# Second attention: the shared experts' second product with the activations stationary, and the rank bank moved

## The reference, cut to what matters

```python
x = x + L0_xattn(layernorm(x), ctx)      # softmax attention, 16 heads
x = x + L0_ffn(layernorm(x))             # 8 experts, top 2
x = x + L1_xattn(layernorm(x), ctx)      # attention with softmax on q and k, no score matrix
x = x + L1_ffn(layernorm(x))             # 8 experts, top 2, and 2 shared experts

# in L1_ffn
sh = gelu(einsum('td,sdh->sth', xf, sW1) + sb1[:, None, :])      # 2 shared, hidden 512
shared = (einsum('sth,shd->std', sh, sW2) + sb2[:, None, :]).mean(axis=0)
gates = xf @ rW + rb                                             # top 2 of 8, softmax of the two
out = shared + moe
```

## Time and profile before

| | |
|---|---|
| median of 3 runs | 737.65 us (734.78 to 743.04) |
| the profiled execution | 741.51 us, span 739.5 us |
| busy in the span | PE 677.2 us, DVE 476.6, POOL 380.2, ACT 316.1 |
| mean granted clock of PE | 0.949 |

### The profile page before, as it was taken

How to read it: one execution, slowest core, us unless ns; L and a number is a source line. 1 busy time by engine, 2 the same in 40 slices (tenths; PEclk the granted TensorE clock), 3 DMA queues, 4 the chain that set the end, 5 groups by cost and what they waited for, 6 DMA issues and landing times.

```text
span 739.5 us, 15744 instructions
## 1 busy us (share of the span) xinstructions
PE 677.2 (92%) x5140; PEld 503.8 (68%) x5140; DVE 476.6 (64%) x1380; ACT 316.1 (43%) x665; POOL 380.2 (51%) x502
## 2 busy tenths in 40 slices
PE   7999999999998889999978799999999799999990
PEld 3566666666667669899956455555554499999990
DVE  3576887878787758887756777777565233333336
ACT  3444455445433233232213366666654344444440
POOL 5313175576557625666740277666655245545552
PEclk9999999999999779999996899999999799999996
DMA  6811111120201558988790000000001778877769
GB/s 174 268 19 10 11 29 28 25 36 19 36 20 37 153 138 266 268 265 260 216 257 0 1 29 30 23 23 26 31 25 41 217 238 262 272 240 228 229 209 285
DMA packets 102119, 91.34 MB, mean 124 GB/s; under 512 B 52952, under 2 KB 85848, under 8 KB 101720
## 3 DMA queue, kind: packets, MB, share of 16 engines
q1 hardware_dynamic: 86375, 68.80, 34.3%
q0 software_dynamic: 8640, 17.84, 6.8%
q10 hardware_dynamic: 7025, 3.70, 1.8%
HBM read 69.13 MB, written 22.72 MB: 124 GB/s over the span
## 4 chain that ended last, share of the span: by engine, by line
PE 68%; DVE 14%; DMA 6%; ACT 4%; issue 3%; POOL 2%; SPq 2%; POOLq 0%; DVEq 0%; ACTq 0%
PE pair L1373 38%; PE pair L1679 11%; PE pair L1376 8%; PE pair L1731 5%; DVE sm L1126 4%; DVE smax L1122 4%; DMA xr<-xs_sorted 2%; PE pair L1479 2%; DMA y_tok<-ysb,xr 2%; PE pair L1494 2%; DMA xa<-y_tok 1%; PE pair L1414 1%; PE pair L1410 1%; POOL y_tok L629 1%; DVE bns L1072 1%
## 5 line engine op out<-in xcount | busy, mean ns | idle before, releaser
L629 POOL DMA_INDIRECT y_tok<-ysb,xr x142 | 136.3, 960 | 121.9 <-DVE ysb L1042 93.1
L556 POOL DMA_INDIRECT xs_sorted<-xa,slot_i x128 | 131.3, 1026 | 89.1 <-DVE slot_i L949 54.1
L1373 PE MATMUL pair<-xT,w_all 128*128 128x256 f32 (+1 forms) x640 | 139.9, 363 | 0.0
L1373 PEld LDWEIGHTS pair<-xT,w_all 128*128 128x128 f32 x640 | 110.4, 198 | 9.6
L1679 PEld LDWEIGHTS pair<-w_all,hT 128*128 128x128 f32 x852 | 107.1, 193 | 3.6 <-issue 0.4
L1679 PE MATMUL pair<-w_all,hT 128*128 128x128 f32 x852 | 108.8, 276 | 0.2 <-DVE hT L1029 0.2
L806 ACT ACTIVATE hT<-pair,w_all 128x256 f32<-128x256 f32 (+1 forms) x160 | 62.7, 447 | 76.3 <-PE pair L1373 75.6
L1021 DVE COPY xT<-pair 128x256 f32<-128x256 f32 (+1 forms) x80 | 31.5, 394 | 94.1 <-PE pair L1376 87.2
L1373 PE MATMUL pair<-xeT_all,w_sh 128*128 128x512 f32 x128 | 69.4, 625 | 0.0
L823 ACT ACTIVATE hS<-pair,w_sh 128x512 f32<-128x512 f32 x64 | 44.0, 687 | 55.9 <-PE pair L1373 55.1
L1122 DVE TENSOR_REDUCE smax<-pair 128x8 f32<-128x616 f32 x64 | 50.4, 788 | 25.7 <-PE pair L1373 25.2
(11 more groups left out here) (199 smaller groups left out, 1119.5 us busy)
## 6 DMA issues: line engine op xcount, KB each, us to landing
w_all<-in_w SPq DMA_DIRECT2D x40, 578.0 KB
w_all<-in_w SPq DMA_DIRECT2D x40, 450.0 KB
xa<-y_tok SPq DMA_DIRECT2D x32, 256.0 KB, 5.2
xr<-xs_sorted SPq DMA_DIRECT2D x62, 130.0 KB
y_tok<-ysb,xr POOLq DMA_INDIRECT x142
xs_sorted<-xa,slot_i POOLq DMA_INDIRECT x128
out<-x_sb ACTq DMA_DIRECT2D x8, 256.0 KB, 3.5
xs_sorted<-in_pads SPq DMA_DIRECT2D x12, 130.0 KB, 4.3
```

The lines of the kernel that those rows point to most:

```text
L556: g.indirect_dma_start(xs_dram[l], bass.IndirectOffsetOnAxis(ap=slot_i[:, i:i + 1], axis=0), xa[:, GT * c + j // TOPK, j % TOPK, :], None) ...
L629: g.indirect_dma_start(y_dram[l], bass.IndirectOffsetOnAxis(ap=xr[u % NXR][:, t, P:P + 1].bitcast(I32), axis=0), ysb[u % NYB][:, t, :], None)\
L1373: return mm(out_, l_, r_, start=True, stop=True)
```

## The change: what it does

The second product exchanges its operands: the activations `hS` are the weights (128 hidden x 128 tokens, four tiles), a 128x128 block of `w_sh` streams through, and the result has tokens on its partitions. The four tiles share a bank; only the first product of a group opens it. Groups alternate between banks 6 and 7. ACT's copy and PE's transposes go. DVE scales and adds the bank to `x_sb`, then adds the bias, which is now laid out over 128 partitions and 128 columns in `w_sh` (and prepared there once). The ranks of this layer move to bank 2, which `nums` uses too: `values(u)` waits for the slots of group `u - 2`, and the column sum of `u - 1` comes behind `out_turned(u)`, the ranks behind the up-projection of `fill(12)`. For the last group both stay where they were. Ahead of the second routed part PE waits for the add of group 6, whose bank it takes.

```diff
-WSC = NSH * B1 + NSH * NC1 + NSH
+WSC = NSH * B1 + NSH * NC1 + NSH * P
...
         def rank_bank(l):
-            return bank[6 + l]
+            return bank[6 - 4 * l]
...
-                def shared_out(u):
-                    act.wait_ge(S("sdown_step"), NC1S * (u + 1))
...
-                    s_.activation(yS[u % 2][:], bank[6][:], ACT.Identity, bias=sb2[:], scale=1.0 / NSH)\
-                        .then_inc(S("sy_ready"), 1)
...
             def shared_add(g):
-                dve.wait_ge(S("sT_done"), g + 1)
-                xg = x_sb[:, GT * g:GT * (g + 1), :].rearrange("p t d -> p (t d)")
-                v.tensor_tensor(xg, xg, bank[7][:], ALU.add).then_inc(S("sx_added"), 1)
+                dve.wait_ge(S("sdown_step"), NC1S * (g + 1))
+                xg = x_sb[:, GT * g:GT * (g + 1), :]
+                link(v.scalar_tensor_tensor(xg, bank[6 + g % 2].rearrange("p (t d) -> p t d", d=P), 1.0 / NSH, xg,
+                                            ALU.mult, ALU.add))
+                v.tensor_tensor(xg, xg, sb2.unsqueeze(1).to_broadcast([P, GT, P]), ALU.add).then_inc(S("sx_added"), 1)
...
                     if c == 0:
-                        after(pe, S("sy_ready"), g)
+                        after(pe, S("sx_added"), g - 1)
                     wd = s * B1 + UP + k * P
-                    mm(bank[6][:], w_sh[:, wd:wd + P], hS[i % 4][:], start=(c == 0), stop=(c == NC1S - 1))\
-                        .then_inc(S("sdown_step"), 1)
-
-                def shared_turn(u):
-                    pe.wait_ge(S("sy_ready"), u + 1)
-                    pe.wait_ge(S("slots"), NCH + min(u + 2, NGRP))
-                    after(pe, S("sx_added"), u)
                     for t in range(GT):
-                        last = turn(tile(bank[7], t), tile(yS[u % 2], t))
-                    last.then_inc(S("sT_done"), 1)
+                        last = mm(tile(bank[6 + g % 2], t), tile(hS[i % 4], t), w_sh[:, wd:wd + P],
+                                  start=(c == 0 and t == 0), stop=(c == NC1S - 1 and t == GT - 1))
+                    last.then_inc(S("sdown_step"), 1)
...
                 def values(u):
...
+                    if u > 1:
+                        pe.wait_ge(S("slots"), NCH + u - 1)
...
                     fill(8, 9)
-                    if live(u - 1):
-                        after(pe, S("sx_added"), u - 2)
-                        column_sums(1, u - 1)
+                    if u == NGRP:
+                        column_sums(1, U_LAST)
                     fill(10, 11)
+                    if u == NGRP:
+                        ranks(1, U_LAST)
                     if live(u):
                         out_turned(u)
-                    if live(u - 1):
+                    if live(u - 1) and live(u):
+                        column_sums(1, u - 1)
+                    fill(12)
+                    if live(u - 1) and live(u):
                         ranks(1, u - 1)
-                    fill(12)
                     if live(u):
                         project(u)
-                    if live(u - 2):
-                        shared_turn(u - 2)
                     fill(13, 14, 15)
             attention1()
+            pe.wait_ge(S("sx_added"), NGRP - 1)
             pe.wait_ge(S("emap"), 2)
             routed(1)
```

More of the change, by code:

```diff
@@ L240, in build @@
         w_sh = sb("w_sh", [P, WSC])
-        sb2 = sb("sb2", [P, 1])
+        sb2 = w_sh[:, NSH * (B1 + NC1):NSH * (B1 + NC1) + P]
         cst = sb("cst", [P, K_N])
@@ L833, in turned @@
                     copy_out(dst, bank[0][:]).then_inc(S(name), 1)
-                def shared_out(u):
-                    act.wait_ge(S("sdown_step"), NC1S * (u + 1))
-                    if u == 0:
-                        act.wait_ge(S("sb2_ready"), 1)
-                    after(act, S("sT_done"), u - 1)
-                    s_.activation(yS[u % 2][:], bank[6][:], ACT.Identity, bias=sb2[:], scale=1.0 / NSH)\
-                        .then_inc(S("sy_ready"), 1)
                 for u in range(-1, NGRP + 2):
@@ L867, in attention1 @@
                     gelu(u, 8)
-                    if live(u - 2):
-                        shared_out(u - 2)
                     gelu(u, 10)
@@ L1247, in shared_bias @@
                 dve.wait_ge(S("ws_in"), 16)
-                sbc = NSH * (B1 + NC1)
-                link(v.tensor_tensor(sb2[:], w_sh[:, sbc:sbc + 1], w_sh[:, sbc + 1:sbc + 2], ALU.add))
-                v.tensor_scalar(sb2[:], sb2[:], 1.0 / NSH, None, ALU.mult).then_inc(S("sb2_ready"), 1)
+                sbc = NSH * (B1 + NC1) + P
+                link(v.tensor_tensor(sb2, sb2, w_sh[:, sbc:sbc + P], ALU.add))
+                link(v.tensor_scalar(sb2, sb2, 1.0 / NSH, None, ALU.mult))
             def attention1():
@@ L1863 @@
                         + [cols(i[M1 + "sb1"])[s] for s in range(NSH)]
-                        + [cols(i[M1 + "sb2"])[s] for s in range(NSH)], axis=1)
+                        + [np.broadcast_to(i[M1 + "sb2"][s][None, :], (P, P)) for s in range(NSH)], axis=1)
     wa = np.concatenate([i[n][:, None] for n in (A0 + "bq", A0 + "bk", A0 + "bv", A1 + "bv")]
```

## The result

The changed kernel takes 742.56 us (median; 736.26 to 745.94), the one before, run beside it, 738.38 (733.52 to 744.57): a ratio of 1.0048, 95% interval 1.0029 to 1.0066 (the quotient of the two medians is 1.0057; the ratios in this text are estimates with an interval and need not be that quotient). The changed kernel is slower by about half a per cent. The forecast, 741.1 for a median of 737.65, is a ratio of 1.0047. The profiled executions can't be set against each other as wholes: the one after has the longer loop and is shorter, 740.42 us (span 738.4) against 741.51, since its loop began some 6 us earlier. The first transposes of the exponentials stand at 389.00 instead of 395.37 (in the other profiles of this study, with either form of the loop, between 391.9 and 395.9), those of group 1 at 408.60 instead of 414.52.

A forecast was written before the change was run, and what follows sets the result against it. PE looked like the bound, with a second path through DVE, POOL and ACT only 0.22 us slack. 0.50 + 0.8 + 1.1 + 0.9 + 0.16 = +3.5 us on 737.65 gave 741.1 us; range 732.1 to 747.7.

The forecast's parts named there:

- The second product's step: PE, shared experts' second product with operands exchanged: +0.04 us for each of 64 steps, +0.32 per group.
- The rival of weight loads that aren't hidden: PE, second product: six more loads each paid like a product, +0.66 a step, +42 us, 780; chance 0.02.
- Transposes go, PE's balance -0.11 per group: PE, each group: four transposes saved, -0.43 us, against +0.32 for the second product's steps.
- The new waits cost nothing: Second attention: products waiting for earlier groups' slots or add, and the wait ahead of the routed part, cost nothing.
- Slots 1.0 later, half swallowed by the third scatter, 0.22 of slack: DVE to POOL to ACT: scatters end 0.50 us later; after slack the exponential comes +0.28 per hand-over.
- PE alone is the bound: Second attention loop: later slots don't matter, so 734.6 us with free steps or 736.9 with dearer ones; chance 0.25.
- the scatters are caught again: POOL, third scatter held off by DVE's bias add: total +6.5 us, 744.2, or +7.5, 745.2; chance 0.23.
- The last group's kept input +0.9: Last group, DVE's kept input feeding PE's transposes: some 0.1 us spare, no bias add beside the scatters, +0.9.
- Four dearer steps +0.16: PE, last group, from the kept input's transposes to its ranks: four dearer second-product steps, +0.16 us.
- one at +0.8: One loop hand-over where the third scatter already takes 0.96 us, so nothing is swallowed: 1.0 - 0.22 = +0.8.
- The first hand-over, +0.50: First group-to-group hand-over of the second attention loop: no slack, so the scatters' whole +0.50 us is lost.
- the clock as a rival: PE's half-clock stretch ahead of the routed part: return one or two us sooner or later, 1.5 us either side.

The follow-up runs named there:

- order_alone: Kernel before with only the column sums and ranks moved later (shared transposes half a step later): 743.73 us against 739.53, ratio 1.0050.
- no_bias_add: Changed kernel without DVE's second add, so the shared experts' second bias is missing: 741.62 us, ratio 1.0036 to the kernel before.
- the split alone: Changed kernel with two instead of three scatters ahead of the next inverse deviation on POOL: 738.36 us, ratio 0.9992 to the kernel before.
- tail_early: Changed kernel with two scatters ahead of the inverse deviation (one in the last group) and the last group's transposes, logits, sums and ranks earlier: 734.75 us, ratio 0.9950.

## Why the prediction was right

The forecast followed the right path: the sums and ranks come later, POOL's scatters with them, and DVE's query reaches ACT behind the end of the table load. That it came out at the measured ratio to the fourth place is luck, since the interval is 1.0029 to 1.0066 and two terms of the sum were wrong. By its steps:

- *The second product's step*: +0.04 to 0.90 (the two rows, 0.85 and 0.90, give 0.05); measured 0.89. The rival of weight loads that aren't hidden (1.5 us a step, 780) fell.
- *Transposes go, PE's balance -0.11 per group*: PE's work per period fell by 0.15.
- *DVE's second add is hidden*: 0.30 of 129.03 us came back when it was taken away, 0.24 of it by a gap elsewhere.
- *The new waits cost nothing*: in the stretch from 409 to 600 PE waited for the copy of the exponentials, once for the kept input, and for the rows' transfers; for nothing new.
- *Slots 1.0 later, half swallowed by the third scatter, 0.22 of slack*: 0.99, 0.50, and 0.26 in the period where I had 0.28. The idle time ahead of the transposes is 0.68, predicted 0.67. The hand-over from DVE to ACT, put at 0.05, took 0.04 (514.66 to 514.70). The residual and the moments did move, by 0.14 (the bias add stands 5.22 behind the output's end instead of 5.08). "PE alone is the bound" (no later than before) fell by order_alone, "the scatters are caught again" by the 0.96 of every third scatter within the loop.
- *The last group's kept input +0.9*: 0.91. *Four dearer steps +0.16*: 0.19.

Two terms of "the sum" were mis-sized.

The "one at +0.8" is not one period but two, and each loses less. I read the 0.96 of the third scatter at 490.82 as "nothing is swallowed here" and kept the shift of 1.0. But that scatter was clear of the add because DVE's slots were late in that very period; and in another period the third scatter had lost only part of the 0.50. DVE's rows of the first and POOL's row of the second, kernel before:

```profile
486.80 0.15 DVE L943 COPY pre<-pair 1x1 f32<-1x1 f32 x1 [0.92 <-PE pair L1394]
486.98 0.23 DVE L944 TENSOR_TENSOR posn<-pair,cst 128x64 f32<-128x64 f32 x1
```

```profile
532.41 1.28 POOL L556 DMA_INDIRECT xs_sorted<-xa,slot_i  x1 [0.31 <-issue]
```

In two groups only, a small copy (`pre`) stands ahead of the steps that make the slots. In the first of these, before, that copy came late (an idle time of 0.92, against 0.59); after it is prompt. From the output's transposes to the slots it was 1.48 (485.50 to 486.98) and is 2.34 (481.07 to 483.41): a shift of 0.86, where its neighbours have 1.20 (0.99 to 2.19 in the period of the earlier trace rows). So this hand-over loses the usual 0.26, plus 0.50 that isn't swallowed, minus 0.34: 0.42; measured 0.46. In the second, the scatter of before had lost only 0.32 (1.28 for 0.96), so 0.18 less is swallowed, and the slots shift by 1.43 (from 528.58 - 527.38 = 1.20 to 526.29 - 523.66 = 2.63), 0.23 more: 0.26 + 0.18 + 0.23 = 0.67; measured 0.69. The 0.23 is DVE's gap of 0.26 behind the small copy, shown above with no_bias_add. Together 1.15 in place of 0.8 + 0.28: the two errors nearly cancel. Why DVE is late at the copy or behind it in one period and kernel and not in another stays open; PE's ranks ahead of it show no gap.

The first hand-over, +0.50, came out at +1.18. The clock makes up most of the rest. Ten microseconds from that group's transposes on, before and after:

```profile
414.52:424.52 10.00, 10.00 (x35) 6.49 (x36) 6.73 (x27) 5.90 (x10) 1.34 (x3) 0.66 0.01 2
```

```profile
408.60:418.60 10.00, 10.00 (x38) 7.69 (x39) 5.85 (x21) 5.63 (x10) 1.35 (x3) 0.59 0.01 2
```

The granted clock is 0.66 and 0.59 in them, so 0.7 us of full-speed work are missing; the output's transposes come 9.04 us behind instead of 8.61, while later periods have 7.70 for 7.91: 0.64 from the clock, which leaves 0.54 for the order, predicted 0.50. A profile with the same PE stream confirms the size: in the split alone the clock is 0.66 there, and the output's transposes come 8.41 behind, 0.63 less than in the kernel after. The prediction had the clock as a rival, but at the start of the routed part.

The order of the products can't have lowered this clock. In the kernel after it is 1.00 up to 406.5 us and 0.50 from 407 on: it falls while PE stands idle (405.98 to 408.60). PE's stream is the old one up to the first of the up-projections at 413.32, behind which the column sum used to stand:

```profile
405.32 0.66 PE L1368 MATMUL pair<-cst,xa 128*128 128x128 f32 x4 [1.64 <-DVE xa L1274]
408.60 1.08 PE L1368 MATMUL pair<-cst,wide 128*128 128x128 f32 x4 [2.63 <-ACT xeT_all L663]
...
413.32 3.59 PE L1365 MATMUL pair<-xeT_all,w_sh 128*128 128x512 f32 x4
```

The same code can get either value: the split alone and tail_early do not differ there, their clocks are 0.66 and 0.58, their hand-overs 21.32 and 22.11. But the four profiles with the old order have 0.66 to 0.68, and of the six with the new order five have 0.58 to 0.61; with so few, whether the changed program meets the lower value more often stays open.

Without the clock's 0.64 the way to the list lost 3.56 us, against 3.5 in the forecast.

## What to carry to other kernels

Look for the second path that closes within a few tenths of the busiest engine's period, and write its slack down: here PE was 99% busy, and an edit that cut PE's work still made the kernel slower, since it moved a small product (the ranks) whose result a whole in-order queue was waiting for. What stands behind that result in the queue decides: one transfer fewer ahead of POOL's small computation (the inverse deviation) undid the loss, one more cost its full 1.26 us in every hand-over. And at the end of a loop put the work that the next part waits for ahead of the filling: that was worth more than the change itself, in either kernel.

## What I had not expected of the hardware

The length of a scatter's issue on POOL depends on what DVE has begun just before, and an experiment made for something else shows it. Last group, kernel after, DVE and POOL:

```profile
556.21 0.69 DVE L1054 TENSOR_TENSOR x_sb<-x_sb,w_sh 128x512 f32<-128x512 f32 x1
```

```profile
556.32 1.42 POOL L556 DMA_INDIRECT xs_sorted<-xa,slot_i  x1 [0.30 <-issue]
```

The same scatter in no_bias_add, where that add is gone:

```profile
560.34 0.97 POOL L556 DMA_INDIRECT xs_sorted<-xa,slot_i  x1 [0.31 <-issue]
```

It begins 0.11 us behind an add with two inputs from SBUF and takes 1.42; without the add 0.97. In the loop of the kernel after, a scatter begun 0.37 ahead of such an add (507.21, the add at 507.58) keeps its 0.96.

The ten profiles give the size. Behind the start of a DVE step of 0.66 to 0.69 us that reads two tensors from SBUF, a scatter takes 1.46 when it begins 0.03 later, 1.42 at 0.11, 1.28 at 0.21, 1.12 at 0.41, and its plain 0.96 from 0.56 on. So it loses what is left of that step, less about 0.13. When both begin within 0.03 it can go the other way: the scatter keeps 0.96 and the DVE step takes 0.73 to 0.75. An add of the same length whose second input is a PSUM bank costs a scatter nothing; kernel before, DVE and POOL:

```profile
498.26 0.68 DVE L1062 TENSOR_TENSOR x_sb<-x_sb,pair 128x512 f32<-128x512 f32 x1
```

```profile
498.27 0.96 POOL L556 DMA_INDIRECT xs_sorted<-xa,slot_i  x1 [0.30 <-issue]
```

That is why the shift of the slots could be half swallowed, and why it was not swallowed alike in every period.
